# Latent attention on one core: probabilities turned by VectorE and DMA instead of TensorE, attention unrolled

## The reference, cut to what matters

```python
xn = layernorm(x)
q = (xn @ wq.T).reshape(B, S, 16, 192);  q_nope, q_pe = q[..., :128], rope(q[..., 128:])
kv = xn @ wkv_a.T;  kv_cache, k_pe = rmsnorm(kv[..., :128], kv_norm_w), rope(kv[..., 128:])
q_lat = einsum('bshd,hdc->bshc', q_nope, wkv_b_h[:, :128])
scores = (q_lat . kv_cache + q_pe . k_pe) * 192 ** -0.5, masked causally
attn = softmax(scores)
out_lat = einsum('bsht,btc->bshc', attn, kv_cache)
out = einsum('bshc,hdc->bshd', out_lat, wkv_b_h[:, 128:])
result = x + out.reshape(B, S, 2048) @ wo.T + (xn @ ternary(w_ffn).T + b_ffn)
```

## Time and profile before

| what | value |
|---|---|
| median of 3 runs | 1972.43 us (1972.4 to 1973.72) |
| profiled execution, span | 1972.3 us |
| TensorE busy | 1911.1 us, 97% |
| VectorE busy | 1277.8 us, 65% |
| ScalarE busy | 887.7 us, 45% |
| GpSimd busy | 317.0 us, 16% |
| DMA | 147.46 MB, mean 75 GB/s |
| mean granted TensorE clock | 0.989 |

### The profile page before, as it was taken

The page is one execution under the profiler, slowest core; times in us unless marked ns, Lnnn a source line. Parts: engine busy times, 40 slices in busy tenths (PEclk is TensorE's granted clock), DMA queues, the critical chain, the costliest instruction groups (busy, mean ns, idle before and its releaser), DMA issues.

```text
span 1972.3 us, 32409 instructions
## 1 busy us (share of the span) xinstructions
PE 1911.1 (97%) x10414; PEld 1596.1 (81%) x10414; DVE 1277.8 (65%) x3031; ACT 887.7 (45%) x1646; POOL 317.0 (16%) x313
## 2 busy tenths in 40 slices
PE   5999899999999999999999999999999999999998
PEld 4887677778888888888888888878888888888886
DVE  5665566666666666666666676666666566666665
ACT  4444344444444444444444444444444444444443
POOL 4565222221111111111001110010010110101100
PEclk9898999999999999999999999999999999999999
DMA  5896322233111112210101011212000010011000
GB/s 181 314 311 219 109 95 85 96 128 107 63 64 53 53 64 96 97 54 32 53 32 43 32 53 42 76 34 74 22 32 32 31 43 21 32 32 34 19 11 22
DMA packets 53076, 147.46 MB, mean 75 GB/s; under 512 B 4834, under 2 KB 17379, under 8 KB 51492
## 3 DMA queue, kind: packets, MB, share of 16 engines
q1 hardware_dynamic: 52208, 145.71, 21.7%
q10 hardware_dynamic: 820, 1.15, 0.2%
HBM read 112.23 MB, written 34.60 MB: 74 GB/s over the span
## 4 chain that ended last, share of the span: by engine, by line
PE 81%; DVE 4%; issue 3%; POOL 2%; ACT 0%; DVEq 0%; POOLq 0%; ACTq 0%
PE p_score L996 31%; PE p_out L1025 18%; PE p_tr L1013 12%; PE p_lat L976 7%; PE p_tr L1036 6%; PE p_rot L976 4%; DVE rot_sin L1108 2%; PE p_out L1036 2%; DVE probs L1081 1%; PE p_score L1000 1%; POOL qp_l L1247 1%; POOL qp_l L1250 1%; POOL rotated L1236 1%; DVE pT_l L1093 0%; DVE rot_cos L1104 0%
## 5 line engine op out<-in xcount | busy, mean ns | idle before, releaser
L1173 ACT ACTIVATE pT_h<-p_tr 128x512 fp32r<-128x512 f32 (+3 forms) x640 | 339.0, 531 | 790.6 <-PE p_tr L1013 788.5
L1081 DVE TENSOR_SCALAR_CACHE_REDUCE probs<-p_score 128x512 f32<-128x512 f32 (+3 forms) x640 | 388.7, 607 | 168.6 <-PE p_score L996 109.7
L1093 DVE TENSOR_TENSOR pT_l<-p_tr,pT_h 128x512 fp32r<-128x512 f32 (+3 forms) x640 | 390.4, 610 | 159.5 <-ACT pT_h L1173 152.7
L1013 PE MATMUL p_tr<-ident,probs 128*128 128x128 f32 x2176 | 343.0, 273 | 0.0
L1164 ACT ACTIVATE probs<-probs,neg_max 128x128 f32<-128x128 f32 (+15 forms) x256 | 307.5, 1201 | 70.3 <-DVE neg_max L1087 69.0
L1013 PEld LDWEIGHTS p_tr<-ident,probs 128*128 128x128 f32 x2176 | 260.4, 140 | 52.5
L1025 PE MATMUL p_out<-pT_h,V_h 128*128 128x512 f32 (+3 forms) x640 | 274.7, 429 | 6.8 <-DVE pT_l L1093 6.8
L996 PE MATMUL p_score<-Kn_h,q_h 128*128 128x512 f32 (+3 forms) x640 | 241.3, 377 | 3.3 <-DVE q_l L1115 3.3
L996 PE MATMUL p_score<-Kp,qp_h 128*128 128x512 f32 (+3 forms) x640 | 234.5, 366 | 8.6 <-POOL qp_l L1250 8.6
L1025 PE MATMUL p_out<-pT_h,V_l 128*128 128x512 f32 (+3 forms) x640 | 234.9, 367 | 0.0
L1025 PE MATMUL p_out<-pT_l,V_h 128*128 128x512 f32 (+3 forms) x640 | 233.5, 365 | 0.0
(11 more groups left out here) (143 smaller groups left out, 2676.4 us busy)
## 6 DMA issues: line engine op xcount, KB each, us to landing
Wq<-wq_scr SPq DMA_DIRECT2D x62, 512.0 KB, 3.3
Wv<-wv_scr SPq DMA_DIRECT2D x62, 512.0 KB, 3.2
Wp<-wp_scr SPq DMA_DIRECT2D x31, 512.0 KB, 3.3
wq_scr<-Wq SPq DMA_DIRECT2D x16, 512.0 KB, 5.3
wv_scr<-Wv SPq DMA_DIRECT2D x16, 512.0 KB, 5.3
xT_scr<-xT SPq DMA_DIRECT2D x3, 2048.0 KB, 10.1
xT<-xT_scr SPq DMA_DIRECT2D x3, 2048.0 KB, 7.8
x_in<-in_x SPq DMA_DIRECT2D x4, 1024.0 KB, 7.0
```

The costliest lines, as they stand in the source:

```text
L1013: mm = pe.transpose(p_tr[k % PT_RING][:, i * P:(i + 1) * P], probs[p][:, i, k * P:(k + 1) * P], ident[:, :])
L1081: dve.tensor_scalar(probs[p][:, i, b * CW:b * CW + width], p_score[u % 2][:, 0:width], SCALE, LOWEST, ALU.mult, ALU.max, accum_out=part_ma ...
L1093: dve.tensor_tensor(pT_l[r][:, cols], p_tr[r][:, cols], pT_h[r][:, cols].bitcast(F32), ALU.subtract).then_inc(pT_split, 1)
L1173: act.activation(pT_h[r][:, cols], p_tr[r][:, cols], ACT.Copy).then_inc(pT_high, 1)
```

## The change

The 128x128 transposes of TensorE go. A row block of probabilities (`probs`, now one row block per buffer, three buffers) is turned by VectorE in 32x32 blocks (`turn_row`, into `turned`, three buffers), stored to DRAM scratch `p_scr` (`store_row`), and loaded back by four DMAs of 32 partitions each (`load_rows`, once for rows 0 to 2, once for row 3), which puts each 32-key block on its partitions of `pT`. In chunks 2 and 3 the loads come in two parts of half the key tiles. ScalarE makes the high part of two key tiles at a time (`high_group`), GpSimd the low part, in place (`low_group`), where VectorE did it before. All loops of the attention are written out (`for g in range(HEADS + 2)`, g being chunk x 16 + head).

A step g now has: scores of head g, latent projection of g+1 and output projection of g-2 in the first four units, values of g-1 from unit 6 on (`LEAD = 6`, `values_by`), in chunk 0 after all units. Score buffers in PSUM are three instead of two, result tiles two. `Wq`, `Wv`, `acc`, `cosT` and `sinT` have one buffer in attention instead of two. SP's order per step is `step` of the sync block below. A turned row i of head g is due in unit (i+1)(j+1), plus 1 where j > 0 (`row_due`); row 3 in the next step.

```diff
-PT_RING = 3
+SCORE_RING = 3
+ROW_RING = 3
+HIGH_RING = 3
+QR = 4
+LEAD = 6
+HEADS = NCH * H
...
+def values_by(cur, prev, u):
+    units, tiles = tiles_of(cur), tiles_of(prev)
+    if chunk_of(cur) == 0 or u < LEAD:
+        return 0
+    return min(tiles, -(-tiles * (u - LEAD + 1) // (units - 1 - LEAD)))
+def groups_ahead(cur, prev, u):
+    ahead = min(u + 2, tiles_of(cur) - 1)
+    return (values_by(cur, prev, ahead) + 1) // 2
...
+def parts_of(g):
+    return 1 if chunk_of(g) < 2 else 2
+def part_tiles(g, part):
+    width = tiles_of(g) // parts_of(g)
+    return width * part, width * (part + 1)
+def in_by(g, part):
+    return 16 * 2 * QR * ((g - (2 * H if part else 0)) // 2 + 1)
+def free_by(g, end):
+    if chunk_of(g) < 2:
+        return tiles_before(g - 1) if g >= 2 else 0
+    if g == 2 * H:
+        return tiles_before(g)
+    return tiles_before(g - 1) + min(tiles_of(g - 1), end)
+def row_due(cur, i):
+    j = chunk_of(cur)
+    return (i + 1) * (j + 1) + (1 if j else 0)
...
+        probs = [sb(f"probs{i}", [P, S]) for i in range(ROW_RING)]
+        turned = [sb(f"turned{i}", [P, 4, NT, 32]) for i in range(ROW_RING)]
+        pT = sb("pT", [P, QB, 4, NT, 32], F32R)
+        pT_h = [sb(f"pT_h{i}", [P, QB, 4, 2, 32], F32R) for i in range(HIGH_RING)]
...
+        by_query = t["p_scr"].rearrange("s i p a n -> s i p a n")
+        by_key = t["p_scr"].rearrange("s i (r k) a n -> s a k (i r) n", r=QR)
...
+        def group(g, k):
+            first = QB // 2 if k == groups_of(g) - 1 else 0
+            return slice(tile_base(g) + 2 * k, tile_base(g) + 2 * k + 2), slice(first, QB)
...
+            def store_row(g, i):
+                row = QB * g + i
+                sp.wait_ge(blocked, row + 1)
+                if i == 0:
+                    for part in range(parts_of(g - 2) if g >= 2 else 0):
+                        sp.wait_ge(turned_in[part][g % 2], in_by(g - 2, part))
+                sp.dma_start(by_query[g % 2, i, :, :, 0:32 * tiles_of(g)],
+                             turned[row % ROW_RING][:, :, 0:tiles_of(g), :].rearrange("p a t q -> p a (t q)")
+                             ).then_inc(turned_out[i], 16)
+            def load_rows(g, rows, part):
+                first, end = part_tiles(g, part)
+                for i in range(rows.start, rows.stop):
+                    sp.wait_ge(turned_out[i], 16 * (g + 1))
+                need(sp, pv_done, free_by(g, end))
+                for a in range(4):
+                    to = pT[32 * a:32 * (a + 1), rows, :, tile_base(g) + first:tile_base(g) + end, :]
+                    sp.dma_start(to.rearrange("p i r t q -> p (i r) (t q)").bitcast(F32),
+                                 by_key[g % 2, a, :, QR * rows.start:QR * rows.stop, 32 * first:32 * end]
+                                 ).then_inc(turned_in[part][g % 2], 16)
...
+                early, last = slice(0, QB - 1), slice(QB - 1, QB)
+                if 1 <= g <= HEADS:
+                    if parts_of(g - 1) > 1:
+                        load_rows(g - 1, early, 1)
+                    store_row(g - 1, QB - 1)
+                    for part in range(parts_of(g - 1)):
+                        load_rows(g - 1, last, part)
+                if g + 2 < HEADS:
+                    load_q(g + 2)
+                if g >= 2 and g <= HEADS:
+                    load_v(g - 1)
+                if g % 2 and g + 3 < HEADS:
+                    load_rotary(g + 3)
+                if g < HEADS and j + 1 < NCH and h == H - 2:
+                    load_tables(j + 1)
+                    load_chunk(j + 1)
+                if g < HEADS:
+                    for i in range(QB - 1):
+                        store_row(g, i)
+                        if j and h == 1 and i == 1:
+                            store_chunk(j - 1)
+                            load_residual(j)
+                    load_rows(g, early, 0)
...
+            def values(g, k):
+                n = groups_before(g) + k // 2
                 if k == 0:
...
+                if k % 2 == 0:
+                    pe.wait_ge(p_low, n + 1)
+                last = k == tiles_of(g) - 1
+                i = slice(max(0, k - QB * chunk_of(g)), QB)
+                high, low = pT_h[n % HIGH_RING][:, i, :, k % 2, :], pT[:, i, :, tile_base(g) + k, :]
+                cols = slice(P * i.start, CW)
+                for a, (v, pt) in enumerate(((V_h, high), (V_l, high), (V_h, low))):
+                    mm = pe.matmul(p_out[:, cols], v[:, k, :], pt, start=(k == 0 and a == 0),
...
+                    if u == 0 and g % 2 and g + 1 < HEADS:
+                        project_rotary(g + 1)
+                    if u < QB and g >= 2:
+                        project_out(g - 2, u)
+                    if u < IT and g + 1 < HEADS:
+                        project_latent(g + 1, u)
+                    if 1 <= g < HEADS:
+                        for k in range(done, values_by(g, g - 1, u)):
+                            values(g - 1, k)
+                            done = k + 1
+                if 1 <= g <= HEADS:
+                    for k in range(done, tiles_of(g - 1)):
+                        values(g - 1, k)
...
+            def turn_row(g, i):
+                row, tiles = QB * g + i, QB * chunk_of(g) + i + 1
+                dve.wait_ge(exped, row + 1)
+                if row < ROW_RING:
+                    dve.wait_ge(cleared, row + 1)
+                else:
+                    dve.wait_ge(turned_out[(row - ROW_RING) % QB], 16 * ((row - ROW_RING) // QB + 1))
+                for first in range(0, tiles, 8):
+                    t8 = slice(first, min(first + 8, tiles))
+                    rows = probs[row % ROW_RING][:, P * t8.start:P * t8.stop]
+                    last = dve.transpose(turned[row % ROW_RING][:, :, t8, :].rearrange("p a t q -> p t a q"),
+                                         rows.rearrange("p (t a q) -> p t a q", a=4, q=32))
+                last.then_inc(blocked, 1)
...
+                    if 1 <= g <= HEADS and u == (1 if chunk_of(g - 1) else 0):
+                        turn_row(g - 1, QB - 1)
+                    if g >= 2 and u >= 1 and u <= QB - 1:
+                        accumulate(g - 2, u - 1)
+                    if g % 2 and g + 1 < HEADS:
+                        for op in ((), (0,), (1, 2), (3, 4))[u] if u < 4 else ():
+                            rotate(g + 1, op)
+                    if g >= 2 and u == min(QB, units - 1):
+                        accumulate(g - 2, QB - 1)
+                    if u == min(5, units - 1) and g + 1 < HEADS:
+                        split_query(g + 1)
+                    for i in range(QB - 1):
+                        if g < HEADS and u == row_due(g, i):
+                            turn_row(g, i)
+                if 1 <= g <= HEADS:
+                    split_output(g - 1)
+                    invert(g - 1)
...
+            def high_group(g, k):
+                n = groups_before(g) + k
+                tiles, i = group(g, k)
+                for part in range(parts_of(g)):
+                    if 2 * k == part_tiles(g, part)[0]:
+                        act.wait_ge(turned_in[part][g % 2], in_by(g, part))
+                need(act, pv_done, 2 * (n - HIGH_RING + 1))
+                act.activation(pT_h[n % HIGH_RING][:, i, :, :, :].rearrange("p i r t q -> p (i r) (t q)"),
+                               pT[:, i, :, tiles, :].bitcast(F32).rearrange("p i r t q -> p (i r) (t q)"),
+                               ACT.Copy).then_inc(p_high, 1)
...
+                    if 1 <= g < HEADS:
+                        for k in range(done, groups_ahead(g, g - 1, u)):
+                            high_group(g - 1, k)
+                            done = k + 1
+                    if g < HEADS and (u + 1) % (chunk_of(g) + 1) == 0:
+                        exp_row(g, u // (chunk_of(g) + 1))
+                    if u == 4 and g + 1 < HEADS:
+                        high_query(g + 1)
+                        high_rotary(g + 1)
+                if units == QB and g + 1 < HEADS:
+                    high_query(g + 1)
+                if 1 <= g <= HEADS:
+                    for k in range(done, groups_of(g - 1)):
+                        high_group(g - 1, k)
+                if units == QB and g + 1 < HEADS:
+                    high_rotary(g + 1)
+                if 1 <= g <= HEADS:
+                    high_output(g - 1)
...
+            def low_group(g, k):
+                n = groups_before(g) + k
+                tiles, i = group(g, k)
+                pool.wait_ge(p_high, n + 1)
+                need(pool, qp_ready, 2 * min(g + 2 if k < 2 else g + 3, HEADS))
+                low = pT[:, i, :, tiles, :].rearrange("p i r t q -> p (i r) (t q)")
+                high = pT_h[n % HIGH_RING][:, i, :, :, :].rearrange("p i r t q -> p (i r) (t q)")
+                pool.tensor_tensor(low, low.bitcast(F32), high.bitcast(F32), ALU.subtract).then_inc(p_low, 1)
+            def step(g):
+                if g % 2 and g + 1 < HEADS:
```

(15 more changed lines are left out.)

461 lines of the change are left out of this document (167 added, 294 removed).

## The result

The changed kernel takes 2792.97 us (median of 4 runs, 2785.97 to 2798.05) against 1973.08 for the kernel before, run beside it: a ratio of 1.415 (95% interval 1.413 to 1.417), 42% slower.

A forecast was written before the change was run, and what follows sets the result against it. The prediction took TensorE, busy 97% of the span, to bound the kernel before. From 1972 us, longer heads added 438 and a longer end 30, together 2440 us; range 2100 to 2820.

The forecast's parts named there:

- what is taken away: All 2176 turnings leave TensorE, 239 us of its chain; the low part leaves VectorE, which frees nothing by itself.
- Each new step's cost: Estimated prices of VectorE's turning, ScalarE's high part, GpSimd's low part, the DMA transfers and SP's issues.
- The order of SP: On SP, row 3's store queues behind three quarters of the head's loads; TensorE stalls 8 us in chunk 1.
- B's floor: Rival B: landing chain hidden, GpSimd's low groups alone set the pace in attention; about 1950 us, chance 0.07.
- Chunk 0's circle: In chunk 0, SP's stores and loads close a circle of two heads, 31.9 us, so 16.0 us each.
- The end: After the last scores, the remaining work takes 52 us against 22, +30 us.
- The stall's clock at nothing: TensorE's lower clock after a stall mostly hidden behind GpSimd's pace, put at nothing; 100 us if not hidden.
- Unrolled streams at nothing: Instruction fetches for the written-out loops put at nothing; 2 us a head would be +115 us.
- Rival C: Loads writing only 32 partitions run at half of 340 GB/s, 438 us over 2360; 2800 us, chance 0.15.
- The likeliest case: The whole kernel slows to 2440 us, own range 2230 to 2640; chance 0.63.
- Rival D: DMA issues on SP cost 1.23 us each, +154 us, 2590 us; counted within the likeliest case's range.
- A: Rival: stores, loads and splits hidden behind scores and projections, so the straight gain shows; 1733 us, chance 0.06.

The follow-up runs named there:

- e3: Changed kernel with only SP's order altered: row 3's store and the first part's last loads ahead of the second part's early loads; 2603.33 us.
- e1: Changed kernel with each load of probabilities filling all 128 partitions instead of 32, same bytes, values computed in wrong order; 2646.99 us.
- e4: Changed kernel without any store or load of the probabilities, pT filled once with other numbers; 2363.59 us.
- e8: Changed kernel with 18, 30, 38 and 44 extra matmuls on TensorE before a head's first value tile in chunks 0 to 3; 2799.66 us.
- e5: e4 with GpSimd's low part cut to 32 columns instead of up to 1024; 2113.77 us.
- e13: e5 with two high copies ahead of row 0's exponential and, from chunk 1, the next query's halves ahead of the probabilities' groups; 2209.23 us.

## Why the forecast was low, step by step

- *What bounds before* and *what is taken away* hold: 239 us left TensorE.
- *Each new step's cost* was near: turning 1.24 us for 8 tiles (1.21 ns a column, 1.11 taken), high 1.05 (1.1 taken), low 2.37 and 1.29 (2.6 and 1.4 taken), issue 0.45 (eight in 3.62 us; 0.43 taken).
- *The order of SP* was right in kind and in price (e3). The time of its early loads was undersized: they ran at 213 to 216 GB/s, below the 261 taken as the lower bound.
- *The heads, in the terms of the sum.* The first value tile runs 22.9, 25.7 and 29.7 us after the end of the last score block in chunks 1 to 3 (21.5, 21.9 and 25.7 forecast for the first low group). That is 147 us over the kernel, about what e1 gives back for the rate (146). What follows it in a head takes 17.1, 18.2 and 24.9 us (12.9, 16.3 and 22.6 forecast), 134 us. Chunk 0 has 22.2 for 16.0, 99 us. Together they are the miss of the heads, (160.6 - 136.9) x 16 = 379 us.
- *The step that failed is B's floor*: that without the landing chain TensorE would reach its values at 13.5 to 14.3 us and only GpSimd's pace would follow, 14.0, 26.4, 30.1 and 36.9 us a head. e4 measures 22.2, 32.0, 35.8 and 45.0, (135.0 - 107.4) x 16 = 442 us more. The forecast put at nothing the wait of the output projection for `o_l` (3.11 us in every second head of chunk 3), the wait for `acc` behind it (1.2), and the rotary sum ahead of the low parts (2.58). Its transfers stand for 490 us in the sum (2440 - 1950) and cost 429 (2793 - 2364), so 61 us too many hide part of the failed floor.
- *Chunk 0's circle* was the wrong circle: 16.0 forecast for SP's, 22.2 measured with or without transfers. It runs over the last exponential, the query's high half, the high copies, 3.6 us of low parts and 2.6 of rotary halves, and the values behind a stall of 4.34 or 5.90 us, in turn, at the slower clock.
- *The end*, +30 in the sum, is not there: (160.6 - 109.5) x 16 = 818 us of heads leave 2 of the 820 for everything else.
- *The stall's clock at nothing*: by the sum of busy time it is 259 us, and e8, which lifts the mean from 0.843 to 0.932, gets nothing back. The estimate stands for the time, but TensorE's busy time of "about 1650" does not (1931).
- *Unrolled streams at nothing*: no run isolates them. The waits and the slow clock below already account for all of e5's excess, which leaves little room for them.
- *Rival C* gave the number, 2800, by 360 us for slow loads. Slow they were, 213 to 216 GB/s, though not down to half of 340 (170), but their price was under half (146), and the engines' chain made up the rest. Its sign, over 2.5 us of bytes for 0.39 MB, did not show: at 214 GB/s they take 1.8.
- *That 2793 lies within 2100 to 2820 is luck.* The likeliest case ended at 2640, the upper end stood there for C, and neither had the chain of the engines that e4 shows. Of the signs, TensorE's stall once a head (6.4 to 13.1 us in chunks 1 to 3), ended by the low group, and SP's wait for its own store came true; the periods did not.
- *Rival D*: issues cost 0.45 us, not 1.23. *A* is not reached even by e5.

What stays open is how e5's remaining 2114 - 1733 = 381 us divide. The waits for `o_l`, `acc`, `pT` and the query's low half on TensorE are 83 + 37 + 122 + 13 = 255 us there, the slow clock 1808 - 1672 = 136; which of these would return if another went was not tried, and e13 warns against adding them.

No version here beats the kernel before. The turning on TensorE cost 0.11 us a tile and left the other engines room (VectorE was busy for 65% of the span, GpSimd for 16%); its replacement hands every probability from VectorE to SP, by way of DRAM to ScalarE, to GpSimd and to TensorE.
